# High parts of keys and queries kept on chip for the shift stage, bounds eight blocks behind the scores

## The reference

```python
h = _layernorm(x) * (1 + ca) + sa
q = (h @ Wq + bq).reshape(b, s, H, HD).transpose(0, 2, 1, 3)
k = (h @ Wk + bk).reshape(b, s, H, HD).transpose(0, 2, 1, 3)
mask = cols <= rows + WINDOW                  # WINDOW = 128
scores = jnp.where(mask, q @ k.T / sqrt(HD), -inf)
attn = jax.nn.softmax(scores, axis=-1)
x = x + ga * ((attn @ v) @ Wo + bo)
...                                           # second norm, router, 8 experts, top 2
```

## Time and profile before

| what | value |
|---|---|
| median of 3 runs | 2013.33 us (2011.85 to 2013.97) |
| the profiled execution | 2015.3 us, span 2013.5 us |
| mean granted TensorE clock | 0.938 of full speed |
| PE busy | 1776.0 us, 88% of the span |
| ACT busy | 1577.0 us, 78% |
| DVE busy | 612.1 us, 30% |
| POOL busy | 290.5 us, 14% |
| DMA | 116.63 MB, mean 58 GB/s |

### The profile page before, as it was taken

One profiled execution on the slowest core, in us unless ns is written; L12 is line 12 of the kernel. 1 busy time (PEld: TensorE's weight loads), 2 busy tenths in 40 slices (PEclk: granted clock), 3 DMA queues, 4 the chain that ended last, 5 costly groups with the idle time before them and its releaser, 6 DMA issues. The chain is left out here.

```text
span 2013.5 us, 46788 instructions
## 1 busy us (share of the span) xinstructions
PE 1776.0 (88%) x18707; PEld 1000.5 (50%) x18707; DVE 612.1 (30%) x1436; ACT 1577.0 (78%) x2074; POOL 290.5 (14%) x333
## 2 busy tenths in 40 slices
PE   4953999999999998999999999676189999999995
PEld 3832333333333333333333333355178888888884
DVE  4964000000000000000000000245366677667662
ACT  2732899998999998999999999322178888888883
POOL 1000100001100011000020000146412222222221
PEclk9975999999999999999999999766599999999997
DMA  4455400004000022000010000565332222222223
GB/s 141 157 150 126 91 10 10 10 10 91 18 10 10 10 49 51 18 10 10 5 31 10 10 2 2 208 231 199 112 91 37 37 37 37 38 38 38 38 38 97
DMA packets 84187, 116.63 MB, mean 58 GB/s; under 512 B 9468, under 2 KB 75964, under 8 KB 83388
## 3 DMA queue, kind: packets, MB, share of 16 engines
q1 hardware_dynamic: 66920, 90.84, 16.1%
q0 software_dynamic: 13296, 17.80, 5.2%
q10 hardware_dynamic: 3760, 5.03, 0.9%
HBM read 72.90 MB, written 40.74 MB: 56 GB/s over the span
## 5 line engine op out<-in xcount | busy, mean ns | idle before, releaser
L1112 ACT ACTIVATE at_probs<-at_scores 128x1536 f32<-128x1536 f32 (+2 forms) x756 | 1022.6, 1435 | 52.7 <-PE at_scores L1013 47.4
L1013 PE MATMUL at_scores<-at_q_rows,kept_k_rows 99*32 99x512 bf16 (+3 forms) x9920 | 616.0, 361 | 32.8 <-ACT at_probs L1112 16.9
L1030 PE MATMUL at_out<-at_probs,kept_v 128*17 128x512 f32 (+3 forms) x4832 | 586.9, 565 | 5.1 <-DVE at_out_T L1125 4.7
L1013 PEld LDWEIGHTS at_scores<-at_q_rows,kept_k_rows 99*32 99x32 bf16 x9920 | 238.0, 96 | 556.5 <-ACT at_probs L1112 344.3
L1125 DVE COPY at_out_T<-at_out 128x512 f32<-128x512 f32 x32 | 22.1, 692 | 967.1 <-PE at_out L1030 967.1
L1790 PE MATMUL ex_ps_y<-kept_w,kept_mixed 128*128 x1136 | 258.8, 381 | 2.9 <-ACT kept_mixed L1851 2.9
L1097 POOL TENSOR_SCALAR_AFFINE_SELECT at_probs<-at_probs 128x512 f32<-128x512 f32 (+2 forms) x156 | 83.4, 543 | 1004.0 <-ACT at_probs L1112 1002.1
L1790 PEld LDWEIGHTS ex_ps_y<-kept_w,kept_mixed 128*128 128x128 f32 x1136 | 211.4, 191 | 29.7 <-issue 3.4
L1851 ACT ACTIVATE kept_mixed<-ex_ps_hT,kept_b 128x128 f32<-128x128 f32 x568 | 154.6, 383 | 78.4 <-PE ex_ps_hT L1782 78.4
L1030 PEld LDWEIGHTS at_out<-at_probs,kept_v 128*17 128x17 f32 x4832 | 127.6, 98 | 130.0 <-DVE at_out_T L1125 20.5
L1876 DVE TENSOR_TENSOR ex_w_low<-kept_w,ex_w_high 128x1024 fp32r<-128x1024 f32 x142 | 167.8, 1222 | 38.9 <-ACT ex_w_high L1824 38.0
(11 more groups left out here) (225 smaller groups left out, 1296.0 us busy)
## 6 DMA issues: line engine op xcount, KB each, us to landing
kept_w<-in_W SPq DMA_DIRECT2D x16, 1024.0 KB, 10.0
kept_mixed<-queue SPq DMA_DIRECT2D x71, 129.5 KB, 2.1
k_parts<-kparts SPq DMA_DIRECT2D x8, 768.0 KB, 3.7
q_parts<-qparts SPq DMA_DIRECT2D x8, 768.0 KB, 3.7
at_q_rows<-q_parts SPq DMA_DIRECT2D x32, 192.0 KB
kept_k_rows<-k_parts SPq DMA_DIRECT2D x4, 1120.0 KB
x_rows<-in_x SPq DMA_DIRECT2D x4, 1024.0 KB, 14.0
kept_k_rows<-k_parts SPq DMA_DIRECT2D x8, 512.0 KB
```

Source lines behind the costliest of these rows:

```text
L1013: ins = nc.tensor.matmul(ps_s[b:b + CT, c % 2, at:at + part], k_rows[:, k + b:k + b + CT], q_rows[:, q:q + part], start=True, stop=True)
L1030: ins = nc.tensor.matmul(ps_o[h * CT:h * CT + HD + 1, first:C], v[:, kb, g * GH + h, :], probs[:, slot, column:column + width], start=i == ...
L1112: nc.scalar.activation(probs[:, c % RING, 0:width], ps_s[:, c % 2, 0:width], ACT.Exp).then_inc(exped, 1)
```

## The change

In stage 1, DVE writes the high part of each chunk into a view of `kept["mixed"]` (its first half for the keys, its second for the queries) and only the middle and low parts into `kparts` and `qparts`, which shrink from three parts to two. SP stores a chunk with two DMAs, one of the high part and one of the other two; the waits count 32 in place of 16.

The shift stage reads the same view. Its 16 loads and all waits for them are gone. Since a head now lies in both halves, `own` has 16 columns in place of 8 and is made by DVE from the identity (a reduce and a copy) in place of three POOL instructions; `first_keys` has 512 columns for each half in place of 256; the two low-score matmuls of a block have 512 columns each and add up in one bank; the squared-length matmuls have 16 columns and add up in pairs. PE's order is new: the squared lengths of block t come behind the low scores of block t + 8, and those of the last 8 blocks behind all low scores.

```diff
+def high_parts(keep, n):
+    half = keep["mixed"][:, n * NT // KD:(n + 1) * NT // KD, :].rearrange("p t d -> p (t d)")
+    return half.bitcast(BF16).rearrange("p (m s) -> p m s", m=KD)
...
-                    sp.dma_start(to.rearrange("(a d) h s -> (d h) a s", a=3 * KD),
+                    sp.dma_start(dram[name][0:HD, :, tokens].rearrange("(a d) h s -> (d h) a s", a=KD),
+                                 high[n][:, :, tokens]).then_inc(kept[u], 16)
+                    sp.dma_start(dram[name][HD:PARTS, :, tokens].rearrange("(a d) h s -> (d h) a s", a=2 * KD),
                                  parts[:, u].rearrange("p a m s -> p (a m) s")).then_inc(kept[u], 16)
...
-                    dve.wait_ge(kept[u], 16 * (c // 2))
-                step.inc(nc.vector.tensor_copy(parts[:, u, 0], full[:]))
+                    dve.wait_ge(kept[u], 32 * (c // 2))
+                step.inc(nc.vector.tensor_copy(top, full[:]))
...
-            load(sp, 1, "q_parts")
...
-            load(act, 0, "k_parts")
...
-                    act.wait_ge(high_in[n][part], 16 * KD)
...
+            def bound_block(t):
+                part = t // BLOCKS
+                pe.wait_ge(squared, 2 * part + 2)
+                for n in range(2):
+                    for m in range(KD):
+                        ins = nc.tensor.matmul(ps_norm[n][:, :, t],
+                                               square[n][:, part % 2, m, t % BLOCKS * P:(t % BLOCKS + 1) * P],
+                                               own[:], start=m == 0, stop=m == KD - 1)
+                if t % BLOCKS == BLOCKS - 1:
+                    ins.then_inc(norms_ready, 1)
...
-                    ins = nc.tensor.matmul(ps_low[:, t % RING, m * HH:(m + 1) * HH, :], high[1][:, m, t * P:(t + 1) * P],
-                                           first_keys[:, m], start=True, stop=True)
+                    ins = nc.tensor.matmul(ps_low[:, t % RING], high[1][:, m, t * P:(t + 1) * P],
+                                           first_keys[:, m], start=m == 0, stop=m == KD - 1)
                 ins.then_inc(low_scored, 1)
+                if t >= BLOCKS:
+                    bound_block(t - BLOCKS)
+            for t in range(NT - BLOCKS, NT):
+                bound_block(t)
...
-            dve.wait_ge(high_in[0][0], 16 * KD)
-            dve.wait_ge(pool_step, 4)
+            nc.vector.tensor_reduce(own_sum[:], ident[:].rearrange("p (d h) -> p h d", d=HH), AX.X,
+                                    ALU.add).then_inc(own_ready, 1)
+            dve.wait_ge(own_ready, 1)
+            nc.vector.tensor_copy(own[:], own_sum[:]).then_inc(own_ready, 1)
+            dve.wait_ge(own_ready, 2)
```

More of the change, by code:

```diff
@@ L134, in attention_inputs @@
         qf = sb("qf", [P, KD, C], F32)
-        kparts = sb("kparts", [P, 2, 3, KD, C], BF16)
-        qparts = sb("qparts", [P, 2, 3, KD, C], BF16)
+        high = [high_parts(keep, n) for n in range(2)]
+        kparts = sb("kparts", [P, 2, 2, KD, C], BF16)
+        qparts = sb("qparts", [P, 2, 2, KD, C], BF16)
         ones = sb("ones", [P, P], F32)
@@ L194, in _ @@
                     sp.wait_ge(parts_ready, 2 * c + n + 1)
-                    to = dram[name][0:PARTS, :, c * C:(c + 1) * C]
-                    sp.dma_start(to.rearrange("(a d) h s -> (d h) a s", a=3 * KD),
+                    tokens = slice(c * C, (c + 1) * C)
+                    sp.dma_start(dram[name][0:HD, :, tokens].rearrange("(a d) h s -> (d h) a s", a=KD),
+                                 high[n][:, :, tokens]).then_inc(kept[u], 16)
+                    sp.dma_start(dram[name][HD:PARTS, :, tokens].rearrange("(a d) h s -> (d h) a s", a=2 * KD),
                                  parts[:, u].rearrange("p a m s -> p (a m) s")).then_inc(kept[u], 16)
@@ L199, in _ @@
             for u in range(2):
-                sp.wait_ge(k_stored[u], 16 * (NC // 2))
-                sp.wait_ge(q_stored[u], 16 * (NC // 2))
+                sp.wait_ge(k_stored[u], 32 * (NC // 2))
+                sp.wait_ge(q_stored[u], 32 * (NC // 2))
         @block.gpsimd
@@ L425, in split @@
                 u = c % 2
+                top = high[n][:, :, c * C:(c + 1) * C]
                 dve.wait_ge(kq_kept, (2 * c + n + 1) * KD)
                 if c >= 2:
-                    dve.wait_ge(kept[u], 16 * (c // 2))
+                    dve.wait_ge(kept[u], 32 * (c // 2))
+                step.inc(nc.vector.tensor_copy(top, full[:]))
+                step.wait(dve)
+                step.inc(nc.vector.tensor_tensor(full[:], full[:], top, ALU.subtract))
+                step.wait(dve)
                 step.inc(nc.vector.tensor_copy(parts[:, u, 0], full[:]))
                 step.wait(dve)
[L431 to L435, removed]
+                nc.vector.tensor_tensor(parts[:, u, 1], full[:], parts[:, u, 0],
                                         ALU.subtract).then_inc(parts_ready, 1)
@@ L490, in score_shifts @@
         W = BLOCKS * P
-        HH = H // KD
+        HH = P // H
         RING = 4
         SETS = H * NT // P
-        high = [sb(f"sh_high_{n}", [P, KD, S], BF16) for n in "kq"]
+        high = [high_parts(keep, n) for n in range(2)]
         square = [sb(f"sh_square_{n}", [P, 2, KD, W], BF16) for n in "kq"]
         ones = sb("sh_ones", [P, P], F32)
-        own = sb("sh_own", [P, HH], BF16)
-        first_keys = sb("sh_first_keys", [P, KD, HH, FIRST_KEYS], BF16)
+        own = sb("sh_own", [P, H], BF16)
+        own_sum = sb("sh_own_sum", [P, H], F32)
+        first_keys = sb("sh_first_keys", [P, KD, H, FIRST_KEYS], BF16)
         low = sb("sh_low", [P, H, NT], F32)
@@ L517, in score_shifts @@
         ps_turn = psum("sh_ps_turn", [P, SETS, P], F32)
-        high_in = [[sem(f"sh_{n}_in_{m}") for m in range(TOKEN_PARTS)] for n in "kq"]
+        own_ready = sem("sh_own_ready")
         pool_step = sem("sh_pool_step")
@@ L556, in _ @@
         def _(pool):
-            nc.gpsimd.memset(own[:], 1.0).then_inc(pool_step, 1)
             nc.gpsimd.memset(ones[:], 1.0).then_inc(pool_step, 1)
[L560 to L565, removed]
         @block.scalar
         def _(act):
-            load(act, 0, "k_parts")
             for part in range(TOKEN_PARTS):
                 for n in range(2):
-                    act.wait_ge(high_in[n][part], 16 * KD)
                     if part >= 2:
@@ L583, in _ @@
             pe.wait_ge(keys_ready, KD)
+            def bound_block(t):
[8 more added lines that the diff above has]
+                    ins.then_inc(norms_ready, 1)
             for t in range(NT):
-                part = t // BLOCKS
-                if t % BLOCKS == 0:
-                    pe.wait_ge(high_in[1][part], 16 * KD)
                 if t >= RING:
@@ L590, in _ @@
                 for m in range(KD):
-                    ins = nc.tensor.matmul(ps_low[:, t % RING, m * HH:(m + 1) * HH, :], high[1][:, m, t * P:(t + 1) * P],
-                                           first_keys[:, m], start=True, stop=True)
+                    ins = nc.tensor.matmul(ps_low[:, t % RING], high[1][:, m, t * P:(t + 1) * P],
+                                           first_keys[:, m], start=m == 0, stop=m == KD - 1)
                 ins.then_inc(low_scored, 1)
[L594 to L602, removed]
+                if t >= BLOCKS:
+                    bound_block(t - BLOCKS)
+            for t in range(NT - BLOCKS, NT):
+                bound_block(t)
+            pe.wait_ge(pool_step, 1)
             pe.wait_ge(dve_step, 1)
@@ L617, in _ @@
         def _(dve):
-            dve.wait_ge(high_in[0][0], 16 * KD)
-            dve.wait_ge(pool_step, 4)
+            nc.vector.tensor_reduce(own_sum[:], ident[:].rearrange("p (d h) -> p h d", d=HH), AX.X,
[3 more added lines that the diff above has]
+            dve.wait_ge(own_ready, 2)
             for m in range(KD):
                 nc.vector.tensor_tensor(first_keys[:, m],
-                                        high[0][:, m, 0:FIRST_KEYS].unsqueeze(1).to_broadcast([P, HH, FIRST_KEYS]),
-                                        own[:].unsqueeze(2).to_broadcast([P, HH, FIRST_KEYS]),
+                                        high[0][:, m, 0:FIRST_KEYS].unsqueeze(1).to_broadcast([P, H, FIRST_KEYS]),
+                                        own[:].unsqueeze(2).to_broadcast([P, H, FIRST_KEYS]),
                                         ALU.mult).then_inc(keys_ready, 1)
```

## The result

| | before | changed |
|---|---|---|
| median | 2012.59 us (2007.70 to 2013.97, 4 runs) | 1984.71 us (1982.39 to 1987.14, 4 runs) |
| ratio | | 0.9866, 95% interval 0.9845 to 0.9887 |
| same kernel, runs made later beside the experiments | 2012.26 us (17 runs) | 1986.88 us (4 runs), ratio 0.9876 (0.9862 to 0.9891) |
| profiled execution, span | 2013.5 us | 1985.4 us |

A forecast was written before the change was run, and what follows sets the result against it. DVE bounds stage 1, while the shift stage waits for loads of data once on chip. The terms moved the attention's start from 193.6 to 171.5, a gain of 22.1 us: 1991.2 us against the median, range 1987 to 1999.

The forecast's parts named there:

- rival 1: Shift stage's 32 blocks: PE's clock stays down, 2000 us, or swings between its levels, 1996 us; chance 0.14.
- rival 2: Stack load takes 48 us again, so the attention's first scores wait 2.9 us for it: 1996 us; chance 0.05.
- rival 3: Rounding in another order pushes a value beyond 130, so the skipped row maxima run: about 3440 us; chance 0.01.
- Part 4: Serial chain after the reduces stays 9.0 us; last store lands in 3.1 us (2.8 to 5.0); attention starts at 171.5.
- Part 3: Shift stage's 32 blocks: reduces every 0.60 us, six blocks slowed by the lower clock, +1.5 us (0.9 to 2.8).
- Part 1: End of stage 1: the last chunk's second store costs +0.3 us, between a gain of 0.3 and a loss of 0.6.
- How the numbers follow: Whole kernel: forecast's chance 0.74, own range 1987.5 to 1995.5 us; 8-in-10 range 1987 to 1999 us.

The follow-up runs named there:

- Experiment 4: Changed kernel with SP issuing the stack load only after the second part's squared lengths, about 16 us into the stage; ratio 0.9920.
- experiment 1: The changed kernel run again without any edit; ratio 0.9876.
- 8: Changed kernel with idle PE matmuls, 25 in the skipped row maxima and 30 ahead of the attention's first scores; 1982.72 us, ratio 0.9852.
- 6: Changed kernel with idle PE matmuls in the shift stage's chain, the skipped stage and ahead of the attention's first scores, 70 in each of the latter two; ratio 0.9867.
- experiment 7: Changed kernel with the high parts loaded from memory again, 16 loads of 256 KB in the changed order of rows; 1998.03 us, ratio 0.9920.

## Why the prediction was right and wrong

The mechanism was right and the sizes were wrong: the time of the last landing, the number of slow blocks, and the spread allowed around them. In detail: the stage waited for the loads, DVE paces the blocks once they are gone, and the chain behind them moves as it is. No rival came. The clock neither stayed down nor swung; from 134.9 to 155.4 it was granted in full, while PE was paced by DVE: its blocks came 0.60 us apart (the last two of these lines), where 0.53 was its own pace (the first two).

```profile
137.44 0.59 PE L592 MATMUL sh_ps_low<-sh_first_keys,kept_mixed 128*128 128x512 bf16 x2
...
137.97 0.61 PE L592 MATMUL sh_ps_low<-sh_first_keys,kept_mixed 128*128 128x512 bf16 x2
...
138.57 0.60 PE L592 MATMUL sh_ps_low<-sh_first_keys,kept_mixed 128*128 128x512 bf16 x2
```

I had set a rule against the forecast, that short idle times between groups of matmuls let the clock swing in such a loop (the Trainium skill, TensorE: Matmul & The Clock Gate, A second HAM failure mode: psum-queue depth-cycling). It did not show in this loop of 512 columns and four banks, and neither did its 1996 to 2000 us (rival 1):

```profile
138.00:142.00 4.00, 3.87 (x42) 2.34 (x40) 4.00 (x7) 0.30 (x1) 0.00 (x0) 1.00 0.77 131
142.00:146.00 4.00, 3.87 (x42) 2.45 (x42) 4.00 (x8) 3.41 (x2) 0.00 (x0) 1.00 0.85 193
146.00:150.00 4.00, 4.00 (x42) 2.45 (x42) 4.00 (x8) 3.52 (x2) 0.00 (x0) 1.00 0.48 174
```

The stack load's traffic ran out at about 154, before the stores, where 157 was forecast (rival 2 off), and nothing at the lines of the row maxima ran (rival 3 off). The sizes failed. Up to the attention's start 22.1 us of gain were forecast and 25.2 measured; term by term, in us:

| term | forecast | measured |
|---|---|---|
| start of the shift stage | 130.4 | 130.05 |
| start to first reduce | 3.3 | 133.13 - 130.05 = 3.1 |
| first reduce to end of the last | 20.8 | 148.59 + 4.27 - 133.13 = 19.7 |
| from there to SP's last issue | 9.0 | 161.7 - 152.86 = 8.8 |
| last landing | 3.1 | 2.1 |
| landing to the attention's start | 4.9 | 168.37 - 163.8 = 4.6 |
| attention's start | 171.5 | 168.4 |

The first two points below are the steps that failed; a third and the narrow spread add to them.

- **Part 4, the landing, 1.0 us.** 3.1 us were forecast, between 2.8 and 5.0; 2.1 were measured, outside these bounds. I held the stack load responsible for the 5.0 and still took 2.8 as the floor, though the two shorter landings come from the same busy queue. Experiment 4 and the 2.0 or 2.1 of every run with a quiet queue show it. A bound has to come from a row that is free of the disturbance that the change removes.
- **Part 3, the clock, 1.0 us.** +1.5 us were forecast, between 0.9 and 2.8; 0.5 were measured. Six slow blocks were forecast, two came: PE's clock rose 2.5 us after its first matmul (132.45), below the 3 to 9 that I had read from the earlier trace rows. This term scatters: with the same first blocks there were two again in experiments 1 and 8, but five in 6 and six, as forecast, in 4. What decides it stays open, so on this term the forecast could have been right or wrong by luck.
- **Part 1, the second store, 0.35 us.** The shorter transfer made up for the second issue: the second store was issued 0.36 us after the old one's time and landed in 3.3 us where the whole had needed 3.7. All sixteen second stores did so:

```profile
DMA to landing us min/median/max: 3.3/3.3/3.4
```

- **How the numbers follow, the spread of the rest.** I let the runs move 1 us and the attention 2. One pair of profiles differed by 4.1 us in the attention and by 4.7 in routing without an edit there. The steps up to the attention explain 3.1 us of the 5.8 by which the medians beat the forecast of 22.1 (3.3 in the second comparison), and the three terms above are 2.4 of them; the other 2.7 came from the later blocks, which scatter from profile to profile as told in experiment 1. With all this the low end of the range should have been near 1983, an estimate made with hindsight.

That the loads were the wait was right; that they had to be that slow I took for granted, and nothing in the forecast asked why 4.2 MB moved at half share. Of the 25.1 us, 16.1 stay when the parts are loaded again in the other order (experiment 7, with the lag and the rest of the change), and 9.0 come from keeping them on chip. The lag is worth 1.2 to 2.5 us in the changed kernel and nothing without the rest.

## What to carry to other kernels

Before removing a transfer, look at its DMA share: a load that runs at half share while others wait for it may be mended by the order of its rows, and then the removal is worth much less (here 9.0 us of 25.1). Take the bound of a landing from a stretch with a quiet queue, and look at what is queued ahead of the last store of a block, because it lands behind that. Compare stages between barriers, not whole executions, where an effect of 1% is to be explained.

## What the runs showed of the hardware

- Loads of the same 256 KB in 2 KB packets ran at a DMA share of 0.47 to 0.54 (170 to 204 GB/s) head-major, with 8 heads outermost, and at 0.96 (322 GB/s) in the order of the rows in memory; eight issues of SP took 8.8 and 4.1 us.
- Three stores of 128 KB landed in 2.0 to 2.1 us each on a quiet queue and in up to 10.0 us with a stack load ahead of them.
- PE's clock rose between 2.5 us (changed kernel) and 5.7 us (experiment 4) after the first matmul of the same blocks: two to six of them ran at the lower level.
- The attention, thought to be bound by ACT (busy 1024 us in each run), takes 0.45 us more for each us at the lower clock of PE, over twelve profiles; idle matmuls ahead of it took 3 to 6.5 us off it against experiment 1, but none of this was clear of noise in the whole time.
